# Score copies from unit 0 on, the routing chains cut into pieces over units 0 to 2, and row scatters one unit later

## What is computed

```python
energy = jnp.einsum('bqhd,bkhd->bhqk', q, k)              # 16 heads of 16, 4096 tokens
attn = jax.nn.softmax(energy / jnp.sqrt(jnp.float32(D)), axis=-1)
out = jnp.einsum('bhqk,bkhd->bqhd', attn, v)
scores = jax.nn.softmax(xf @ gate_w.T, axis=-1)           # 8 experts, the best two by scores + gate_b
h = jax.nn.silu((xf @ w1 + b1) * (xf @ w3 + b3))          # per expert, 352 hidden; one more expert sees every token
y = sum over the two chosen of weight * (h @ w2 + b2)
```

## Times and profile of the kernel before

| what | us |
|---|---|
| median of the runs | 2087.84 (2087.46, 2087.84, 2090.09) |
| profiled execution | 2085.35 |
| its span | 2083.4 |
| PE, ACT, DVE, POOL busy | 2059.8, 2000.7, 1375.6, 253.1 |
| matmuls of L931 (values), L918 (scores) | 977.9, 682.9 |
| exponentials L1225, L1217, L1222 | 1311.8 (x1359), 517.9 (x477), 201.4 (x106) |
| copies L1804 | 583.2 (x477) |

### The profile page before, as it was taken

How to read it: one execution, slowest core, us unless ns; L and a number is a source line. 1 busy time by engine, 2 the same in 40 slices (tenths; PEclk the granted TensorE clock), 3 DMA queues, 4 the chain that set the end, 5 groups by cost and what they waited for, 6 DMA issues and landing times.

```text
span 2083.4 us, 38786 instructions
## 1 busy us (share of the span) xinstructions
PE 2059.8 (99%) x15722; PEld 975.0 (47%) x15722; DVE 1375.6 (66%) x2037; ACT 2000.7 (96%) x2122; POOL 253.1 (12%) x260
## 2 busy tenths in 40 slices
PE   8999999999999999999999999999999999999998
PEld 6734444444444444444444444444444444444442
DVE  8555666666666666767666767666766665677772
ACT  6799999999999999999999999999999999999998
POOL 0306764000000000000000000000000000033320
PEclk9999999999999999999999999999999999999999
DMA  8873433222222213222222232312122222233322
GB/s 297 282 262 117 140 112 103 61 72 57 77 64 64 68 52 84 66 67 69 57 69 64 64 77 53 88 46 80 53 80 64 70 61 67 76 99 88 108 62 68
DMA packets 223354, 187.83 MB, mean 90 GB/s; under 512 B 110471, under 2 KB 192190, under 8 KB 223174
## 3 DMA queue, kind: packets, MB, share of 16 engines
q1 hardware_dynamic: 209350, 148.68, 25.2%
q0 software_dynamic: 12496, 36.34, 5.4%
q10 hardware_dynamic: 1328, 0.33, 0.1%
HBM read 130.21 MB, written 55.05 MB: 89 GB/s over the span
## 4 chain that ended last, share of the span: by engine, by line
PE 82%; ACT 13%; DVE 3%; issue 1%; DMA 1%; SPq 1%; DVEq 0%; ACTq 0%
PE PS L931 38%; PE PS L918 26%; PE PS L943 11%; ACT probs L1225 8%; PE PS L955 6%; ACT probs L1217 2%; ACT probs L1222 2%; DVE stats L1351 0%; DMA qk_parts<-part_a 0%; DVE probs L1804 0%; DVE probs L1375 0%; DVE x_parts L1387 0%; PE PS L822 0%; SPq L515 0%; DVE part_a L1394 0%
## 5 line engine op out<-in xcount | busy, mean ns | idle before, releaser
L1225 ACT ACTIVATE probs<-PS 128x1024 f32<-128x1024 f32 x1359 | 1311.8, 1053 | 45.0 <-PE PS L918 43.6
L931 PE MATMUL PS<-probs,v_head 128*32 128x512 f32 x8192 | 977.9, 598 | 1.4 <-ACT probs L1225 0.8
L1804 DVE COPY probs<-PS 128x1024 f32<-128x1024 f32 x477 | 583.2, 1223 | 431.2 <-PE PS L918 429.8
L918 PE MATMUL PS<-q_ring,k_stack 50*128 50x512 f32 x4096 | 682.9, 433 | 10.2 <-ACT probs L1225 6.0
L918 PEld LDWEIGHTS PS<-q_ring,k_stack 50*128 50x128 f32 x4096 | 334.2, 184 | 497.4 <-ACT probs L1225 340.9
L1217 ACT ACTIVATE probs<-probs 128x1024 f32<-128x1024 f32 x477 | 517.9, 1086 | 1.7 <-DVE probs L1804 1.4
L931 PEld LDWEIGHTS PS<-probs,v_head 128*32 128x32 f32 x8192 | 217.2, 109 | 496.9 <-issue 457.6
L1222 ACT ACTIVATE probs<-PS 128x2048 f32<-128x2048 f32 x106 | 201.4, 1900 | 0.1
L943 PE MATMUL PS<-x_hi,w_hi 128*128 128x256 f32 (+9 forms) x660 | 199.6, 302 | 0.0
L1297 POOL DMA_DIRECT2D slot_y<-y_sb x39 | 27.9, 717 | 1374.1 <-DVE y_sb L1759 1338.7
L943 PE MATMUL PS<-x_lo,w_hi 128*128 128x256 f32 (+9 forms) x660 | 184.2, 279 | 0.0
(11 more groups left out here) (202 smaller groups left out, 1289.4 us busy)
## 6 DMA issues: line engine op xcount, KB each, us to landing
w_raw<-in_w SPq DMA_DIRECT2D x110, 352.0 KB
k_stack<-qk_parts SPq DMA_DIRECT2D x120, 128.0 KB
w_raw<-in_w SPq DMA_DIRECT2D x55, 256.0 KB
q_ring<-qk_parts SPq DMA_DIRECT2D x372, 32.0 KB
qk_parts<-part_a SPq DMA_DIRECT2D x20, 512.0 KB, 5.0
slot_x<-early_sq SPq DMA_DIRECT2D x39, 256.0 KB, 3.2
slot_in<-slot_x SPq DMA_DIRECT2D x156, 64.0 KB, 2.5
slot_y<-y_sb POOLq DMA_DIRECT2D x39, 256.0 KB, 2.5
```

Source lines behind the costliest of these rows:

```text
L918: last = pe.matmul(bank(2 * score_buffer(turn, g) + r), k_stack[rows, kt * P:(kt + 1) * P], q_ring[rows, sweep, i * QC:(i + 1) * QC], star ...
L931: last = pe.matmul(bank(O_BANK)[VW * j:VW * (j + 1), :], v_head[:, kt, :], slot[:, (j % 2) * QC:(j % 2 + 1) * QC], start=(kt == 0), stop=( ...
L1225: nc.scalar.activation(prob_at(h * GH + g), bank(2 * score_buffer(h, g), 2), ACT.Exp, scale=ENERGY_SCALE).then_inc(s_exp, 1)
L1804: V.tensor_copy(prob_at(h * GH + g), bank(2 * score_buffer(h, g), 2)).then_inc(s_moved, 1)
```

## The change

It starts copies and pairs two units earlier; it cuts the chain of `counts` into four pieces in unit 0 (`totals` between down_hi and copy 20, `full_tiles` between copies 23 and 26, `rests` after copy 32, `order_of_rests` after copy 35), moves `places` to unit 1 in three pieces (before copy 8, between copies 23 and 26, after copy 32), and `experts_of_tiles` to unit 2 in two (between copies 23 and 26, after copy 32). In all units copy 32 is now issued ahead of the piece that stands there. Each `scatter` waits for a group 36 later, and `load_shared` is issued one unit ahead of where it was. No arithmetic is added or left out.

```diff
--- before.py
+++ after.py
@@ -59,7 +59,7 @@
 TANH_AT = 41
 MOVED = (2, 8, 17, 20, 23, 26, 29, 32, 35)
 MERGED = (27, 30)
-MOVE_FROM = 2
+MOVE_FROM = 0
 MOVE_TO = 55
 JOINS = 5
 SCATTERS = 3
@@ -1274,7 +1274,7 @@
 
             def scatter(u):
 
-                pool.wait_ge(s_scores, unit_start(1 + u // SCATTERS) + 4 + 10 * (u % SCATTERS))
+                pool.wait_ge(s_scores, unit_start(2 + u // SCATTERS) + 4 + 10 * (u % SCATTERS))
                 rows = y_sb[:, u % 2, :].rearrange("p (t d) -> p t d", t=TPU)
                 pool.wait_ge(s_xs[u % 2], 16 * (u // 2 + 1))
                 for t in range(TPU):
@@ -1301,8 +1301,11 @@
                 pool.wait_ge(s_xd[half], 16 * FIRST)
             load_shared(0)
             load_shared(1)
+            load_shared(2)
             for u in range(SZ + 1):
-                if u + 2 < SA or u + 2 in (SZ, SZ + 1):
+                if u + 3 < SA:
+                    load_shared(u + 3)
+                if u + 2 in (SZ, SZ + 1):
                     load_shared(u + 2)
                 if u == 0:
                     pool.wait_ge(s_pos, 1)
@@ -1577,13 +1580,16 @@
                 link(V.tensor_tensor(t1, sc, oh, ALU.mult))
                 link(V.reduce_sum(weight[:, :, k], t1, axis=AX))
 
-            def counts():
-
-                cnt, full, end, over, start, key, rank, rest, jump = (sizes[:, i, :] for i in range(9))
+            cnt, full, end, over, start, key, rank, rest, jump = (sizes[:, i, :] for i in range(9))
+
+            def totals():
+
                 for e in range(E):
                     last = V.tensor_tensor_scan(cum[:, :, e], ones_sb[:, 0:NT], ranks[:, 1, :, e], 0.0, ALU.mult, ALU.add)
                 link(last)
                 link(V.tensor_copy(cnt, cum[:, NT - 1, :]))
+
+            def full_tiles():
 
                 def tiles_above(lo, dst):
                     link(V.tensor_scalar(over, cnt, -float(lo), None, ALU.add))
@@ -1594,11 +1600,17 @@
                 tiles_above(CH - 0.5, full)
                 tiles_above(E * CH + CH - 0.5, end)
                 link(V.tensor_tensor(full, full, end, ALU.add))
+
+            def rests():
+
                 link(V.tensor_tensor_scan(end, ones_sb[:, 0:E], full, 0.0, ALU.mult, ALU.add))
                 link(V.tensor_tensor(start, end, full, ALU.subtract))
                 link(V.tensor_scalar(rest, full, float(CH), None, ALU.mult))
                 link(V.tensor_tensor(key, cnt, rest, ALU.subtract))
                 link(V.scalar_tensor_tensor(key, key, 2.0 * E, steps_sb[:, 0:E], ALU.mult, ALU.add))
+
+            def order_of_rests():
+
                 link(V.tensor_tensor(cmp_sz[:, :, :], key.unsqueeze(1).to_broadcast([P, E, E]),
                                      key.unsqueeze(2).to_broadcast([P, E, E]), ALU.is_gt))
                 link(V.reduce_sum(rank, cmp_sz[:, :, :], axis=AX))
@@ -1609,25 +1621,34 @@
 
             def places():
 
-                start, rest, jump = (sizes[:, i, :] for i in (4, 7, 8))
                 link(V.tensor_tensor(at, cum, ranks[:, 1, :, :], ALU.subtract))
                 link(V.tensor_tensor(at, at, ranks[:, 0, :, :], ALU.add))
                 link(V.tensor_tensor(t1, at, over_tokens(rest), ALU.is_ge))
                 link(V.tensor_tensor(t1, t1, over_tokens(jump), ALU.mult))
+
+            def moved_places():
+
                 link(V.tensor_tensor(at, at, over_tokens(start), ALU.add))
                 link(V.tensor_tensor(at, at, t1, ALU.add))
-                for k, oh in enumerate((oh1, oh2)):
-                    link(V.tensor_tensor(t1, at, oh, ALU.mult))
-                    link(V.reduce_sum(posf[:, :, k], t1, axis=AX))
+                link(V.tensor_tensor(t1, at, oh1, ALU.mult))
+
+            def chosen_places():
+
+                link(V.reduce_sum(posf[:, :, 0], t1, axis=AX))
+                link(V.tensor_tensor(t1, at, oh2, ALU.mult))
+                link(V.reduce_sum(posf[:, :, 1], t1, axis=AX))
                 V.tensor_copy(pos[:, :, :], posf[:, :, :]).then_inc(s_pos, 1)
 
-            def experts_of_tiles():
-
-                end, rank = (sizes[:, i, :] for i in (2, 6))
-                tiles = steps_sb[0:1, 2 * E:2 * E + ST].unsqueeze(2).to_broadcast([1, ST, E])
+            tiles = steps_sb[0:1, 2 * E:2 * E + ST].unsqueeze(2).to_broadcast([1, ST, E])
+
+            def tiles_below():
+
                 link(V.tensor_tensor(tile_c[:, :, :], tiles, end[0:1, :].unsqueeze(1).to_broadcast([1, ST, E]), ALU.is_ge))
                 link(V.reduce_sum(tile_f[:, :], tile_c[:, :, :], axis=AX))
                 link(V.scalar_tensor_tensor(tile_f[:, :], tile_c[:, :, E - 1], -float(E), tile_f[:, :], ALU.mult, ALU.add))
+
+            def experts_of_tiles():
+
                 link(V.tensor_tensor(tile_c[:, :, :], tiles, rank[0:1, :].unsqueeze(1).to_broadcast([1, ST, E]), ALU.is_equal))
                 link(V.tensor_tensor(tile_c[:, :, :], tile_c[:, :, :],
                                      steps_sb[0:1, 2 * E:3 * E].unsqueeze(1).to_broadcast([1, ST, E]), ALU.mult))
@@ -1822,6 +1843,8 @@
                 after_values(m + 2)
                 join(u, 2)
                 take_values(m + 4)
+                if u == 1:
+                    places()
                 move_scores(u, 8)
                 if real:
                     gate(u, 1)
@@ -1845,16 +1868,22 @@
                 after_values(m + 6)
                 if real:
                     down_hi(u)
+                if u == 0:
+                    totals()
                 take_values(m + 8)
                 move_scores(u, 20)
                 if real:
                     down_lo(u)
-                if u == 0:
-                    counts()
                 after_values(m + 8)
                 take_values(m + 10)
                 move_scores(u, 23)
                 join(u, 1)
+                if u == 0:
+                    full_tiles()
+                if u == 1:
+                    moved_places()
+                if u == 2:
+                    tiles_below()
                 if routed(u + 1):
                     turn_tokens(u + 1)
                 after_values(m + 10)
@@ -1870,15 +1899,19 @@
                 take_values(m + 14)
                 if more:
                     tokens_lo(u + 1)
+                move_scores(u, 32)
                 if u == 0:
-                    places()
+                    rests()
                 if u == 1:
+                    chosen_places()
+                if u == 2:
                     experts_of_tiles()
-                move_scores(u, 32)
                 after_values(m + 14)
                 join(u, 1)
                 take_values(m + 16)
                 move_scores(u, 35)
+                if u == 0:
+                    order_of_rests()
                 after_values(m + 16)
                 join(u, 1)
                 take_values(m + 18)
```

## The result

| what | before | after |
|---|---|---|
| median of the runs | 2087.84 (2087.46 to 2090.09) | 2109.58 (2107.35 to 2111.09) |
| profiled execution | 2085.35 | 2109.58 |
| its span | 2083.4 | 2107.6 |

The ratio is 1.0099 [1.0088, 1.0109]: the change makes the kernel 1% slower, 21.7 us where the forecast was -0.7. The measured time lies far outside the range.

What follows compares the result with a forecast made beforehand. The prediction saw PE and ACT both nearly full, with plain groups losing time in the buffer hand-over between them. Terms -1.1 (unit 0), -0.6 (unit 1), +1.0 (unit 2) gave -0.7, median 2087.1, range 2084.0 to 2090.2.

Steps and rivals of the forecast that it cites:

- the paragraph on POOL and SP: Scatters and loads: scatters 0 to 7 fall one unit later, token loads keep their time, transfers are the same; 0.
- Unit 0, -1.1: Copies and pairs in unit 0 save at most 1.60 us, less 0.5 for late copies; bounds 0 and -1.6.
- The steps on copies 17 and 20: In unit 0, copy 17 comes about 0.2 us late behind the count, copy 20 0.3 late behind `totals`.
- the signs: What ACT's timeline would show, here three groups in 2.75 us at places 18 to 26 of units 0 and 1.
- Unit 1, -0.6: Copies and pairs in unit 1 bring it from 36.06 to 35.45 us, as in unit 17.
- `places` ahead of copy 8: In unit 1, four steps make copy 8 about 1.0 us later, exponential 8 0.6; claimed 0, at worst +0.6.
- Unit 2, +1.0: Expert chain delays the transpose ending the second sweep; value call 64 starts 1.27 us late, 1.0 arrives; bounds 0 and 1.9.
- Unit 4 on, unchanged: Sign that units from 4 on stay unchanged to 0.1 us.
- The rule that speaks against the change: Each copy adds 0.045 us to ACT's sum by reading SBUF; 18 moved groups cost about 0.76, less pairs' return.
- Rival 2: Slower, ACT's own sum is the bound: 0.8 from 18 groups plus call 64's 1.0, +1.8, median 2089.6; chance 0.12.
- Rivals 1 (all hidden): Copies 17 and 20 of unit 0 not late, call 64's stall taken back: -2.3, median 2085.5; chance 0.24.
- 3 (copies do nothing): Copies in units 0 and 1 each come late behind a chain piece, call 64 covered: 0.0, median 2087.8; chance 0.14.

Runs made afterwards that it cites:

- e3: Kernel after, with only load_slots(8) moved on SP into step 7, behind the keys, queries and all weights of unit 8: 2086.00, ratio 0.9996.
- e8: e7 plus down_hi(0) and down_lo(0) ahead of the count wait, and the expert chain's last two steps behind copy 35 of unit 3: 2084.76, ratio 0.9986.
- e9: e3 with MOVE_FROM = 2, so pieces of the chains without the copies in units 0 and 1: profiled execution 2086.78.
- e2: Kernel after with the scatter waits of the kernel before: 2086.15, ratio 0.9995.
- e6: Kernel after with every scatter waiting for a group 24 earlier: profiled execution 2088.59.
- e4: e3, but with load_slots(8) behind the keys and queries of step 6, still ahead of the weights of unit 8: profiled execution 2094.31.
- e5: Kernel after with every scatter waiting for a group 12 earlier: profiled execution 2094.51.
- e7: e3 with the last five steps of the expert chain behind copy 32 of unit 3 instead of unit 2: 2084.92, ratio 0.9987.
- e1: Kernel before with one line changed, each scatter waiting for a group one unit later, load_shared left where it was: 2149.46, ratio 1.0294.
- e10: Kernel before with MOVE_FROM = 0, so copies in units 0 and 1 with the chains whole: profiled execution 2096.40.

## Why the prediction was wrong

- **The failed step** is the paragraph on POOL and SP: "scatters 0 to 7 fall in units 2 to 4 instead of 1 to 3 ... **0**". It counted 8 scatters, the number of early shared units, where there are 16, one per 256 tokens. With 8 the term would have been right: in the kernel after the eighth scatter goes out from 278.4 on, and SP comes to its wait at 326.1. That SP's first wait for scatters is in its step 6 the paragraph had right; it did not ask what stands behind that wait in SP's queue, and feared late loads only for the tokens. With 16 the loss follows: the last scatter moves from place 4 of unit 6 to place 4 of unit 7, so the wait ends a whole unit (34 us) later, and behind it stand the last two key blocks of head 2 and the weights of unit 8. Measured: +21.1, of which 2.9 are the clock. e3 shows that it is the whole of it. No rival held this case either; the slower one was about ACT's sum.
- **Unit 0, -1.1**: -1.11. The steps on copies 17 and 20 were right: the exponential of place 17 starts 1.15 behind that of place 16 (0.90 before) and that of place 20 2.02 behind that of place 18 (1.82 before), so the copies cost 0.25 and 0.2 where I had worked out 0.2 and 0.3; e8 takes the delay of copy 20 away and gains 0.2. Three groups at places 18 to 20 of unit 0 so take 2.99, where the signs had named 2.75 (e8 has 2.76).
- **Unit 1, -0.6**: -0.61. `places` ahead of copy 8 cost nothing at the unit's end, as worked out.
- **Unit 2, +1.0**: +0.74, and +0.10 in unit 3. The place and mechanism were right, the size was over by 0.2: counted from the unit's place 0, the transpose came after 223.50 - 191.09 = 32.41 us, where I had worked out 225.37 - 192.73 = 32.64, and of PE's wait of 0.99 only 0.84 arrived in the two units.
- **Unit 4 on, unchanged**: true to 0.2, where the sign was 0.1 (unit 4 has +0.19; in e3 it has +0.02), but for unit 7 and for what the last section tells. The text had named the sign to look for: "if a unit after 4 changes at all, ... scatters or loads would be what I had overlooked".
- **Sum**: with the wait moved (e3), units 0 to 3 change by -1.15 - 0.60 + 0.74 + 0.09 = -0.9, where the forecast was -0.7, and the ratio 0.9996 [0.9986, 1.0005] agrees with no change that can be told.
- **The rule that speaks against the change** (ACT's price for a source in SBUF) was rightly given little weight: e3 against e9, which differ in the copies and pairs of units 0 and 1 alone, shows them worth -1.15 and -0.61 and not a loss. The dearer start of each exponential (0.95 for 0.90) is real, but copies and pairs together are worth more; how much of that is the buffer that comes free sooner and how much the pairs is not shown. Rival 2, in which ACT's sum is the bound, fell with that, and by its own sign: three groups at places 18 to 26 of unit 1 take 2.76 and 2.75. Rivals 1 (all hidden) and 3 (copies do nothing) fell by unit 2 and by e9.
- **The range** held sums of small terms only. A moved event for which an issuing queue waits cost nothing here as long as it stayed within the room (e2, e6) and 8 to 21 us beyond it (e4, e5, after); a term like that needs its count checked, or an end of its own.

## What to carry to other kernels

When a row of events is shifted, take its length from the loop's bound in the code and find its *last* event: that one releases whoever waits for all of them. Then read what stands behind that wait in the waiting engine's queue and when each of those transfers is needed; the room (12.8 us here) is free, and beyond it each microsecond cost about one here, the lower clock after PE's wait included. If the late data itself is not urgent, move the wait behind the urgent loads: that one edit on SP gave back the whole 21 us.

## What was not expected of the hardware

**A stall costs more than its length.** After 16 us without work the first value call of 24 matmuls took 5.02 us for 2.78, and in all some 2.9 us came on top.

**A lower clock with no idle before it.** In unit 46 of several executions (after, e2, e6, e7, e8; not before, e1, e3, e4, e5, e9, e10) PE, busy without a break, shows this, here in the kernel after (the rows ahead of it are twelve up products of 32 columns, where unit 7 has 256; e3 has the same ones and keeps its clock):

```profile
1746.00 1.34 PE L918 MATMUL PS<-q_ring,k_stack 50*128 50x512 f32 x6
1747.27 4.48 PE L931 MATMUL PS<-probs,v_head 128*32 128x512 f32 x24
1751.68 0.96 PE L918 MATMUL PS<-q_ring,k_stack 50*128 50x512 f32 x6
```

```profile
1747.00:1752.00 5.00, 5.00 (x30) 1.32 (x28) 0.00 (x0) 3.49 (x5) 0.00 (x0) 0.66 0.39 110
```

It makes the unit 1.6 to 1.7 us longer. It comes with the execution and not with the kernel, as far as the records tell: e2 and e3, whose medians agree, fall on either side, and of the eleven executions of e8 the four with a mean clock of 1.000 took 2083.3 to 2083.7 us and the three with 0.998, the profiled one among them, 2085.2 to 2085.9. Its cause is open. Compare such kernels by the unit and not by one span: e7 and e8 carry these 1.7 in the profiled executions, which hides what they gain there. Units 50 and 51 of the kernel after are 1.2 to 1.3 us longer than in the other kernels here, at a full clock; the cause is open.
